# Moving the tile loads of outsb from GpSimd's DMA queue to SyncE's in an attention and FFN kernel on eight cores

## The chip, the cores and the metric

The kernel runs on the 8 cores of one Trainium2 chip. Each core runs the same program on 2 of the 16 batches, and the cores exchange nothing. The metric is the time on the device in microseconds (us), that of the slowest core.

A core has TensorE (PE in the profile), VectorE (DVE), ScalarE (ACT), GpSimd (POOL) and SyncE (SP). Each takes its instructions in order. Transfers between HBM and the core's own memory are issued by SyncE, into the hardware queue q1, or by GpSimd, into the software queue q0; 16 DMA engines serve both. An instruction that waits, a DMA too, holds everything behind it on its engine.

## The reference, cut to what matters

```python
xn = _layernorm(x, axis=-1)                      # x: 16 x 2048 x 1024, float32
# attention-like part, data = xn
sq = jnp.sum(data * data, axis=-1, keepdims=True)
normed = data * jax.lax.rsqrt(jnp.maximum(sq, 1e-12))
sim = jnp.einsum('bnd,bmd->bnm', normed, normed)
counter = jnp.sum(jax.nn.relu(sim), axis=-1, keepdims=True)
counter = jax.nn.softplus(counter @ W1 + b1)     # 2048 x 1024 per batch
a = jnp.concatenate([data, counter], axis=-1) @ W2
# low-rank FFN
P = jnp.einsum('bsd,dr->bsr', xn, U1)            # rank 256
H = jax.nn.gelu(jnp.einsum('bsr,rf->bsf', P, V1) + b1)
f = jnp.einsum('bsr,rd->bsd', jnp.einsum('bsf,fr->bsr', H, U2), V2) + b2
x = x + a + f
```

## The kernel before, in words

The 2048 rows of a batch are cut into 16 tiles `st` of 128 rows (512 KB each) and 4 groups of four tiles. Small helpers return lists of units, each a cost and a function; `mix` interleaves several lists by these costs, and playing the result gives the order of the instructions. `Sched.add` records each instruction with the tiles that it reads and writes, and works out the waits; what is recorded for "SY" is SyncE's queue and what is recorded for "G" is GpSimd's, each in that order.

**Startup (batch 0).** For each group: four tiles of `x` are loaded into `xa`/`xr` on SyncE (L462), one group ahead, and ScalarE takes the sum and the sum of squares (L473, L478), which frees the buffer for the next load. Some 25 small operations (`emit_colmath`, L333 to L376) make mean and scale. Then the same four tiles are loaded again, into `outsb[st % 2]` (`rld`, L741, on GpSimd), VectorE normalizes them (L415 into `ntok`, in group 0 also L445 into `xntok`), TensorE transposes them (L384) and ScalarE copies them out (L396). Blocks of the similarity matrix follow (L494), each reduced on VectorE (L502). The weights come in 18 chunks of 1 MB through two staging buffers `wstage` (L314, on SyncE), and ScalarE (even chunks, L317) or VectorE (odd chunks, L320) casts them. Chunks 0 to 5 are mixed into the startup, 6 to 17 into stage 1 of batch 0.

On SyncE the startup's order is: constants, `xa` tile 0, chunk 0, tiles 1 to 3; tiles 4 to 7; chunk 1; tile 8, chunk 2, tiles 9 to 11; chunk 3; tiles 12 to 15; chunks 4, 5; then chunks 6, 7 and so on. In the order of the list, the loads of outsb (tile n: rld n) stand at these places: rld 0 and 1 after the load of tile 7 and ahead of chunk 1, rld 2 and 3 behind it; rld 4 to 7 between the load of tile 11 and chunk 3; rld 8 and 9 after tile 15, then chunk 4, rld 10 and 11, chunk 5, rld 12 to 15, chunk 6.

**Stages 1 to 5 of each batch.** The rest of the similarity matrix, the FFN (L603, L624, L636), and `fin_units`, which makes an output tile: `gx` loads `x` again into `outsb[st % 2]` (L669, on GpSimd), 19 matmuls for each half add up in a PSUM bank (L677 to L697), VectorE adds the bank onto outsb (L703), and GpSimd stores it (L710). `gx` of tile n waits for the store of tile n-2. On GpSimd the order is store n-1, gx n, and then mostly the load of an `xr` tile (L440). In stages 2 and 3 of batch 0 SyncE loads the tiles of batch 1 into `xa` for their statistics (L462), and in stages 4 and 5 for `nfm` (L409); each waits until its buffer is free. In batch 1 SyncE has no work.

Of the kernel before, what the change touches and what calls it, by code (L numbers as in the profile page):

```python
# [9 lines left out]
AFT = mybir.ActivationFunctionType  # L10
# [6 lines left out]
QLAG = 2  # L17
HBF_N = 4
FIN_ADD_ENG = "V"
CS_ADD_ENG = "V"  # L20
PQ_EVAC_ENG = "V"
CF_POS = 20
# [145 lines left out]
def build_program():  # L168
# [88 lines left out]
    def pool_slot():  # L257
        i = state["pool"] % POOL_N
        state["pool"] += 1
        return pool[i], ("ps", i)  # L260
# [169 lines left out]
        lc, tp = ph1_units2(b, st, slot_buf, slot_key, load_chan, eng, tok)  # L430
        return lc + tp

    def prep_units2(b, st, slot_buf, slot_key, load_chan=None, load_eng="G"):
        p = b % 2
        C = cols
        t = st // 4
        lc = []
        if load_chan is not None:
            def ld():
                A(load_eng, lambda e: e.dma_start(out=slot_buf[:, :],  # L440
                                                  in_=x[b, st * 128:(st + 1) * 128, :]),
                  writes=[slot_key], chan=load_chan, dma=True)
            lc.append((600, ld))
        def cast():
            A("V", lambda e: e.tensor_scalar(out=xntok[st % 4][:, :], in0=slot_buf[:, :],  # L445
                            scalar1=C["invs"][p][:, st:st + 1],
                            scalar2=C["biasB"][p][:, st:st + 1],
                            op0=AluOpType.mult, op1=AluOpType.add),
              reads=[slot_key, ("cmB", p, st)], writes=[("xntok", st % 4)])
        lc.append((600, cast))  # L450
        return lc, [tp_group(xntok[st % 4], ("xntok", st % 4), xnfm[t % 2],
                             ("xnfm", t % 2), st % 4)]
# [34 lines left out]
    def sim_block_unit(b, q, kc, j, nb_, last):  # L487
        def emit():
            bank, bkey = pool_slot()
            vs = vj_slot()  # L490
            state["blkvs", b, q, kc] = vs
            for dc in range(DC):
                A("T", lambda e, dc=dc:
                  e.matmul(bank[:, :],  # L494
                           nfm[:, dc * 2048 + q * 128: dc * 2048 + (q + 1) * 128],
                           nfm[:, dc * 2048 + kc * 512: dc * 2048 + (kc + 1) * 512],
                           start=(dc == 0), stop=(dc == DC - 1)),
                  reads=[("nfm", q // 4), ("nfm", kc)],
                  writes=[bkey], tag=f"sim{b}_{q}_{kc}")
            col = 4 * (q % 4) + j  # L500
            A("V", lambda e:
              e.tensor_scalar(out=vjunk[:, vs * 512:(vs + 1) * 512],  # L502
                              in0=bank[:, :], scalar1=0.0,
                              scalar2=None, op0=AluOpType.max, op1=AluOpType.add,
                              accum_out=cpart[:, col:col + 1]),
              reads=[bkey], writes=[("cp", col), ("vj", vs)])
            if last:
                A("V", lambda e:
                  e.reduce_sum(call[:, q:q + 1], cpart[:, 4 * (q % 4):4 * (q % 4) + nb_],
                               axis=AX.X),  # L510
                  reads=[("cp", 4 * (q % 4) + jj) for jj in range(nb_)],
                  writes=[("call", q)])
        return (4400, emit)
# [150 lines left out]
    def fin_units(b, t):  # L664
        units = []
        for s_ in range(4):
            st = 4 * t + s_
            def gx(st=st):
                A("G", lambda e: e.dma_start(out=outsb[st % 2][:, :],  # L669
                                             in_=x[b, st * 128:(st + 1) * 128, :]),  # L670
                  writes=[("outsb", st % 2)], chan=("QXF", st % 2), dma=True)
            units.append((600, gx))
            for h in range(2):
                def finh(s_=s_, st=st, h=h):
                    bank, bkey = pool_slot()
                    A("T", lambda e:
                      e.matmul(bank[:, :], onesbr[:, :],  # L677
                               b2bf[0:1, h * 512:(h + 1) * 512], start=True, stop=False),
                      reads=[("onesbr",), ("b2bf",)], writes=[bkey], tag=f"Fb2_{b}_{t}_{s_}")
                    for dc in range(DC):  # L680
                        A("T", lambda e, dc=dc:
                          e.matmul(bank[:, :],  # L682
                                   xnfm[t % 2][:, dc * 512 + s_ * 128: dc * 512 + (s_ + 1) * 128],
                                   w2sb[:, dc * 1024 + h * 512: dc * 1024 + h * 512 + 512],
                                   start=False, stop=False),
                          reads=[("xnfm", t % 2), ("w", "w2")],
                          writes=[bkey], tag=f"F{b}_{t}_{s_}")
                    for dc in range(DC):
                        A("T", lambda e, dc=dc:
                          e.matmul(bank[:, :],  # L690
                                   nfm[:, dc * 2048 + t * 512 + s_ * 128: dc * 2048 + t * 512 + (s_ + 1) * 128],
                                   w2sb[:, (8 + dc) * 1024 + h * 512: (8 + dc) * 1024 + h * 512 + 512],
                                   start=False, stop=False),
                          reads=[("nfm", t), ("w", "w2")], writes=[bkey])
                    for rc in range(2):
                        A("T", lambda e, rc=rc:
                          e.matmul(bank[:, :],  # L697
                                   qfm[t % 2][:, rc * 512 + s_ * 128: rc * 512 + (s_ + 1) * 128],
                                   v2sb[:, rc * 1024 + h * 512: rc * 1024 + h * 512 + 512],
                                   start=False, stop=(rc == 1)),  # L700
                          reads=[("qfm", t % 2), ("w", "v2")], writes=[bkey])
                    A(FIN_ADD_ENG, lambda e:
                      e.tensor_tensor(out=outsb[st % 2][:, h * 512:(h + 1) * 512],  # L703
                                      in0=bank[:, :],
                                      in1=outsb[st % 2][:, h * 512:(h + 1) * 512],
                                      op=AluOpType.add),
                      reads=[bkey, ("outsb", st % 2)], writes=[("outsb", st % 2)])
                units.append((9600, finh))
            def store(st=st):
                A("G", lambda e: e.dma_start(out=out[b, st * 128:(st + 1) * 128, :],  # L710
                                             in_=outsb[st % 2][:, :]),
# [16 lines left out]
    for g in range(NT):  # L728
# [8 lines left out]
        for s_ in range(4):  # L737
            st = 4 * g + s_
            rbuf, rkey = outsb[st % 2], ("outsb", st % 2)
            def rld(rbuf=rbuf, rkey=rkey, st=st):  # L740
                A("G", lambda e: e.dma_start(out=rbuf[:, :],  # L741
                                             in_=x[0, st * 128:(st + 1) * 128, :]),
                  writes=[rkey], chan=("QXF", st % 2), dma=True)
            startup.append((600, rld))
            lc, tp = ph1_units2(0, st, rbuf, rkey, load_chan=None, eng=PH1_ENG, evac="S")
            startup.extend(lc)
# [161 lines left out]
```

How the kernel before makes its waits and increments, by code:

```python
    def emit(self, stream, eng, sems):  # L122
        for o in self.streams[stream]:
            if o.drain:
                eng.drain()
            for c, idx in sorted(o.waits.items(), key=lambda kv: str(kv[0])):
                v = self.wait_value(c, idx)
                if v > 0:
                    eng.wait_ge(sems[c], v)
            inst = o.fn(eng)
            if o.marked:
                if inst is None:
                    inst = eng.nop()
                inst.then_inc(sems[o.chan], 16 if o.dma else 1)
# [733 lines left out]
        @block.gpsimd  # L868
        def _(eng):
            sch.emit("G", eng, sems)
            for k in range(3):
                n_store = sch.chan_count.get(("QST", k), 0)
                if n_store:
                    eng.wait_ge(sems[("QST", k)], 16 * n_store)
```

## Time and profile before

| | us |
|---|---|
| median of 2 runs | 1070.17 (1060.68 and 1079.66) |
| the profiled execution | 1062.01 |
| its span on the slowest core (core 4) | 1060.5 |
| the other cores' spans | 1048.9 to 1054.9 |
| mean granted clock of TensorE, core 4 | 0.879 of full speed |

The busy share of an engine is an average over stages with different limits. The chain of waits goes back from the last instruction to what released each step. "Issue" in it is time for which the profile shows no wait. A DMA's time to landing runs from its issue to the semaphore that tells of its end.

### The profile page before, as it was taken

What the parts mean: (1) busy time and instruction counts of PE and PEld (TensorE: products, weight loads), DVE (VectorE), ACT (ScalarE), POOL (GpSimd) and SP (SyncE); (2) the same over time, 40 slices, a digit from 0 to 9 for tenths busy, and PEclk for the clock granted to TensorE, in tenths of its full rate; (3) what the DMA queues carried; (4) which work ended last, traced back from release to release, by engine and by line L of the source; (5) the groups of instructions that cost most, each with busy time, mean ns of one, the idle gap of its engine ahead of it and who ended that gap; (6) DMA issues with size and microseconds to landing.
All of it is one profiled execution on the core that took longest, in us unless ns stands there. A gap on an engine that the chain in (4) does not pass through costs nothing.

```text
span 1060.5 us, 10460 instructions; the slowest of 8 cores (1048.9 to 1060.5 us)
## 1 busy us (share of the span) xinstructions
PE 794.1 (75%) x3592; PEld 344.4 (32%) x3592; DVE 263.8 (25%) x573; ACT 419.9 (40%) x582; POOL 74.0 (7%) x144
## 2 busy tenths in 40 slices
PE   0335566693999399759967985993999399959997
PEld 0212222232444134324433332441344134324442
DVE  1424343331333122321122333322222111111111
ACT  3344522447243724666341001347223623566310
POOL 0000001001000100100000000001000100100001
PEclk9976668896999599959987997996999689969999
DMA  6546434711223223212352221101111112111222
GB/s 188 173 159 214 148 113 143 265 69 40 100 100 119 79 100 120 106 53 80 100 156 83 100 90 49 60 20 41 60 60 61 59 48 72 60 40 40 80 80 100
DMA packets 32486, 101.49 MB, mean 96 GB/s; under 512 B 4401, under 2 KB 9649, under 8 KB 31922
## 3 DMA queue, kind: packets, MB, share of 16 engines
q0 software_dynamic: 16576, 56.65, 15.3%
q1 hardware_dynamic: 15858, 44.17, 13.1%
q8 instruction: 30, 0.49, 0.2%
q14 instruction: 22, 0.18, 0.1%
HBM read 84.01 MB, written 16.78 MB: 95 GB/s over the span
## 4 chain that ended last, share of the span: by engine, by line
PE 66%; ACT 15%; DMA 8%; issue 6%; DVE 4%; SPq 0%; ACTq 0%; DVEq 0%; POOL 0%; POOLq 0%
PE s L494 13%; PE s L682 10%; PE q L636 10%; PE s L690 10%; PE hx L624 5%; PE s L624 5%; PE tb L384 4%; ACT wstage L579 4%; ACT nfm L584 3%; DMA wstage<-W 3%; PE s L697 2%; ACT xnfm L396 2%; PE s L677 2%; ACT nfm L396 2%; DMA outsb<-x 2%
## 5 line engine op out<-in xcount | busy, mean ns | idle before, releaser
L636 PE MATMUL q<-hbf,u2sb 128*128 128x512 bf16 x512 | 156.4, 391 | 29.6 <-ACT hbf L630 29.5
L494 PE MATMUL s<-nfm 128*128 128x512 bf16 x640 | 173.5, 422 | 5.5 <-ACT nfm L396 5.0
L630 ACT ACTIVATE hbf<-s,fb1c 128x512 bf16<-128x512 f32 x128 | 87.8, 686 | 159.9 <-PE s L624 159.7
L630 ACT ACTIVATE hbf<-hx,fb1c 128x512 bf16<-128x512 f32 x128 | 87.8, 686 | 135.2 <-PE hx L624 135.2
L682 PE MATMUL s<-w2sb,xnfm 128*128 128x512 bf16 x512 | 122.3, 382 | 0.0
L703 DVE TENSOR_TENSOR outsb<-s,outsb 128x512 f32<-128x512 f32 x64 | 44.2, 691 | 309.8 <-PE s L697 280.5
L690 PE MATMUL s<-w2sb,nfm 128*128 128x512 bf16 x512 | 121.0, 379 | 0.0
L384 PE MATMUL tb<-identbf,xntok 128*128 128x128 bf16 x384 | 43.7, 284 | 79.4 <-ACT xnfm L396 55.3
L502 DVE TENSOR_SCALAR_CACHE_REDUCE vjunk<-s 128x512 bf16<-128x512 f32 x80 | 55.3, 691 | 190.9 <-PE s L494 190.9
L624 PE MATMUL hx<-pfm,v1sb 128*128 128x512 bf16 x256 | 78.8, 391 | 25.9 <-ACT hbf L630 25.5
L494 PEld LDWEIGHTS s<-nfm 128*128 128x128 bf16 x640 | 65.4, 106 | 94.8 <-issue 39.4
L624 PE MATMUL s<-pfm,v1sb 128*128 128x512 bf16 x256 | 77.2, 383 | 20.4 <-DVE pfm L610 13.5
L636 PEld LDWEIGHTS q<-hbf,u2sb 128*128 128x128 bf16 x512 | 50.7, 100 | 95.3 <-issue 38.8
L384 PE MATMUL tb<-identbf,ntok 128*128 128x128 bf16 x128 | 16.2, 306 | 87.3 <-DVE ntok L415 76.5
L396 ACT COPY nfm<-tb 128x1024 bf16<-128x1024 bf16 x32 | 32.4, 1012 | 119.0 <-PE tb L384 119.0
L690 PEld LDWEIGHTS s<-w2sb,nfm 128*128 128x128 bf16 x512 | 50.1, 98 | 60.4
L682 PEld LDWEIGHTS s<-w2sb,xnfm 128*128 128x128 bf16 x512 | 45.0, 98 | 61.6 <-issue 16.8
L384 PEld LDWEIGHTS tb<-identbf,xntok 128*128 128x128 bf16 x384 | 34.2, 128 | 90.5 <-issue 90.0
L710 POOL DMA_DIRECT2D out<-outsb x32 | 17.3, 541 | 566.3 <-DVE outsb L703 566.3
L396 ACT COPY xnfm<-tb 128x1024 bf16<-128x1024 bf16 x32 | 32.3, 1010 | 55.1 <-PE tb L384 55.1
L579 ACT ACTIVATE wstage<-s,b1c,w1c 128x512 f32<-128x512 f32 x64 | 49.7, 777 | 5.3
L624 PEld LDWEIGHTS hx<-pfm,v1sb 128*128 128x128 bf16 x256 | 24.1, 99 | 60.3 <-issue 34.7
(86 smaller groups left out, 584.5 us busy)
## 6 DMA issues: line engine op xcount, KB each, us to landing
outsb<-x POOLq DMA_DIRECT2D x48, 512.0 KB, 4.9
xa<-x SPq DMA_DIRECT2D x40, 512.0 KB, 3.9
out<-outsb POOLq DMA_DIRECT2D x32, 512.0 KB, 3.0
xr<-x POOLq DMA_DIRECT2D x28, 512.0 KB, 5.8
wstage<-W SPq DMA_DIRECT2D x8, 1024.0 KB, 6.8
wstage<-U SPq DMA_DIRECT2D x5, 1024.0 KB, 7.8
wstage<-V SPq DMA_DIRECT2D x5, 1024.0 KB, 7.7
xr<-x SPq DMA_DIRECT2D x8, 512.0 KB, 5.5
```

The costliest lines, as they stand in the source:

```text
L384: e.transpose(tb[:, dc * 128:(dc + 1) * 128], src[:, dc * 128:(dc + 1) * 128], identbf[:, :]),
L396: e.copy(dst.rearrange("p (c f) -> p c f", c=8)[:, :, st * 128:(st + 1) * 128], tb[:, :].rearrange("p (c f) -> p c f", c=8)),
L494: e.matmul(bank[:, :], nfm[:, dc * 2048 + q * 128: dc * 2048 + (q + 1) * 128], nfm[:, dc * 2048 + kc * 512: dc * 2048 + (kc + 1) * 512], s ...
L502: e.tensor_scalar(out=vjunk[:, vs * 512:(vs + 1) * 512], in0=bank[:, :], scalar1=0.0, scalar2=None, op0=AluOpType.max, op1=AluOpType.add, ...
L579: e.activation(out=e512[dc % 2][:, :], in_=bank[:, :], func=AFT.Exp, scale=w1c[:, dc:dc + 1], bias=b1c[:, dc:dc + 1]),
L584: e.activation(out=nfm[:, dc * 2048 + t * 512: dc * 2048 + (t + 1) * 512], in_=e512[dc % 2][:, :], func=AFT.Ln, bias=1.0, scale=1.0),
L624: e.matmul(bank[:, :], v1sb[:, c * 4096 + fc * 128:c * 4096 + (fc + 1) * 128], pfm[t % 2][:, c * 512:(c + 1) * 512], start=(c == 0), stop= ...
L630: e.activation(out=hbf[fc % HBF_N][:, :], in_=bank[:, :], func=AFT.Gelu_apprx_tanh, scale=1.0, bias=fb1c[:, fc:fc + 1]),
L636: e.matmul([q0, q1][rc][:, :], u2sb[:, fc * 256 + rc * 128: fc * 256 + (rc + 1) * 128], hbf[fc % HBF_N][:, :], start=(fc == 0), stop=(fc = ...
L682: e.matmul(bank[:, :], xnfm[t % 2][:, dc * 512 + s_ * 128: dc * 512 + (s_ + 1) * 128], w2sb[:, dc * 1024 + h * 512: dc * 1024 + h * 512 + ...
L690: e.matmul(bank[:, :], nfm[:, dc * 2048 + t * 512 + s_ * 128: dc * 2048 + t * 512 + (s_ + 1) * 128], w2sb[:, (8 + dc) * 1024 + h * 512: (8 ...
L703: e.tensor_tensor(out=outsb[st % 2][:, h * 512:(h + 1) * 512], in0=bank[:, :], in1=outsb[st % 2][:, h * 512:(h + 1) * 512], op=AluOpType.add),
```

## The change

The loads of outsb, `rld` (16) and `gx` (32), are recorded for SyncE instead of GpSimd, at the same place of the order. `rld` gets a semaphore of its own (QXO). The rest of the diff changes nothing in the program that is built: `RELU_SPLIT` and `FIN_SPLIT` are 0, so the added branches aren't taken and `finh` calls its two halves in turn, with the same cost in `mix`; the new default of `load_eng` is not used, since each caller that loads passes "G".

```diff
+RELU_SPLIT = 0
+FIN_SPLIT = 0
-    def prep_units2(b, st, slot_buf, slot_key, load_chan=None, load_eng="G"):
+    def prep_units2(b, st, slot_buf, slot_key, load_chan=None, load_eng="SY"):
...
             def gx(st=st):
-                A("G", lambda e: e.dma_start(out=outsb[st % 2][:, :],
+                A("SY", lambda e: e.dma_start(out=outsb[st % 2][:, :],
                                              in_=x[b, st * 128:(st + 1) * 128, :]),
                   writes=[("outsb", st % 2)], chan=("QXF", st % 2), dma=True)
...
-                units.append((9600, finh))
+                if FIN_SPLIT:
+                    units.append((4800, finA))
+                    units.append((4800, finB))
+                else:
+                    def finh(finA=finA, finB=finB):
+                        finA(); finB()
+                    units.append((9600, finh))
...
             def rld(rbuf=rbuf, rkey=rkey, st=st):
-                A("G", lambda e: e.dma_start(out=rbuf[:, :],
-                                             in_=x[0, st * 128:(st + 1) * 128, :]),
-                  writes=[rkey], chan=("QXF", st % 2), dma=True)
+                A("SY", lambda e: e.dma_start(out=rbuf[:, :],
+                                              in_=x[0, st * 128:(st + 1) * 128, :]),
+                  writes=[rkey], chan=("QXO", st % 2), dma=True)
```

## Rows read from the trace of the kernel before

**Rows 1.** The page: busy times and its chain by engine.
```profile
PE 794.1 (75%) x3592; PEld 344.4 (32%) x3592; DVE 263.8 (25%) x573; ACT 419.9 (40%) x582; POOL 74.0 (7%) x144
PE 66%; ACT 15%; DMA 8%; issue 6%; DVE 4%; SPq 0%; ACTq 0%; DVEq 0%; POOL 0%; POOLq 0%
```

**Rows 2.** Waits of the whole span: us in total, times, longest.
```profile
DVE outsb L703 <- DMA outsb<-x: 29.3, 5, 7.3
ACT u2sb L317 <- DVE u2sb L320: 26.2, 1, 26.2
DVE ntok L415 <- DMA outsb<-x: 16.5, 7, 5.7
```

**Rows 3.** Busy time by stretch: length, then each engine's, clock, DMA, GB/s.
```profile
215.00:1016.00 801.00, 659.60 (x2998) 285.43 (x2997) 187.07 (x370) 334.38 (x462) 55.77 (x107) 0.89 0.21 73
1016.00:1054.00 38.00, 37.00 (x164) 14.98 (x161) 6.92 (x10) 1.52 (x3) 4.23 (x8) 1.00 0.31 111
```

**Rows 4.** The chain in order of time: start, length, what.
```profile
4.14 12.81 DMA wstage<-U
106.55 5.75 DMA outsb<-x
136.72 3.47 DMA outsb<-x
630.29 6.55 DMA xr<-x
```

**Rows 5.** DMA of 0 to 30 us: GB/s by 0.75 us, issues with time to landing.
```profile
GB/s 0 0 29 92 36 78 372 321 264 314 254 338 288 296 345 279 274 261 306 318 333 258 236 208 147 82 33 0 0 0 0 180 382 137 109 224 218 224 289 208
outsb<-x POOLq DMA_DIRECT2D x2, 512.0 KB, 6.5
wstage<-V SPq DMA_DIRECT2D x1, 1024.0 KB, 8.8
```

**Rows 6.** VectorE in order of time: start, length, operation, [idle before, releaser].
```profile
33.55 0.81 DVE L415 TENSOR_SCALAR ntok<-outsb,c_scaleA,c_biasA 128x1024 bf16<-128x1024 f32 x1
37.90 1.23 DVE L320 CAST v1sb<-wstage 128x2048 bf16<-128x2048 f32 x1 [2.81 <-DMA wstage<-V]
77.43 1.53 DVE L415 TENSOR_SCALAR ntok<-outsb,c_scaleA,c_biasA 128x1024 bf16<-128x1024 f32 x2
105.18 1.53 DVE L415 TENSOR_SCALAR ntok<-outsb,c_scaleA,c_biasA 128x1024 bf16<-128x1024 f32 x2
112.46 0.81 DVE L415 TENSOR_SCALAR ntok<-outsb,c_scaleA,c_biasA 128x1024 bf16<-128x1024 f32 x1 [5.74 <-DMA outsb<-x]
```

**Rows 7.** SyncE's queue in order of time: start, until the last issue, load.
```profile
28.98 0.43 SPq L314 DMA_DIRECT2D wstage<-V  x1
72.86 0.43 SPq L314 DMA_DIRECT2D wstage<-V  x1
97.42 50.62 SPq L314 DMA_DIRECT2D wstage<-U  x4
```

**Rows 8.** DMA issues of 70 to 73 us.
```profile
wstage<-V SPq DMA_DIRECT2D x1, 1024.0 KB, 6.6
```

**Rows 9.** SyncE's queue, 270 to 345 us: the loads for batch 1's statistics.
```profile
275.21 63.23 SPq L462 DMA_DIRECT2D xa<-x  x7
```

**Rows 10.** GpSimd in order of time: stores and loads of outsb.
```profile
302.66 0.54 POOL L710 DMA_DIRECT2D out<-outsb  x1 [18.91 <-DVE outsb L703]
303.19 0.53 POOL L669 DMA_DIRECT2D outsb<-x  x1
629.76 0.54 POOL L710 DMA_DIRECT2D out<-outsb  x1 [15.02 <-DVE outsb L703]
```

**Rows 11.** The page's list of DMA issues: median us to landing.
```profile
outsb<-x POOLq DMA_DIRECT2D x48, 512.0 KB, 4.9
xa<-x SPq DMA_DIRECT2D x40, 512.0 KB, 3.9
out<-outsb POOLq DMA_DIRECT2D x32, 512.0 KB, 3.0
```

More of the change, by code:

```diff
@@ L500, in emit @@
             col = 4 * (q % 4) + j
[L501 to L506, printed above, removed]
+            state["relu_rr"] = state.get("relu_rr", 0) + 1
+            if RELU_SPLIT and state["relu_rr"] % 2 == 0:
+                A("S", lambda e:
+                  e.activation(out=vjunk[:, vs * 512:(vs + 1) * 512], in_=bank[:, :],
+                               func=AFT.Relu, accum_out=cpart[:, col:col + 1]),
+                  reads=[bkey], writes=[("cp", col), ("vj", vs)])
+            else:
+                A("V", lambda e:
+                  e.tensor_scalar(out=vjunk[:, vs * 512:(vs + 1) * 512],
+                                  in0=bank[:, :], scalar1=0.0,
+                                  scalar2=None, op0=AluOpType.max, op1=AluOpType.add,
+                                  accum_out=cpart[:, col:col + 1]),
+                  reads=[bkey], writes=[("cp", col), ("vj", vs)])
             if last:
@@ L673, in fin_units, with finA @@
             for h in range(2):
-                def finh(s_=s_, st=st, h=h):
+                share = {}
+                def finA(s_=s_, st=st, h=h, share=share):
                     bank, bkey = pool_slot()
+                    share["b"] = (bank, bkey)
                     A("T", lambda e:
@@ L687, in finh, with finB @@
                           writes=[bkey], tag=f"F{b}_{t}_{s_}")
+                def finB(s_=s_, st=st, h=h, share=share):
+                    bank, bkey = share["b"]
                     for dc in range(DC):
@@ L707, in finh @@
                       reads=[bkey, ("outsb", st % 2)], writes=[("outsb", st % 2)])
-                units.append((9600, finh))
+                if FIN_SPLIT:
+                    units.append((4800, finA))
+                    units.append((4800, finB))
+                else:
+                    def finh(finA=finA, finB=finB):
+                        finA(); finB()
+                    units.append((9600, finh))
             def store(st=st):
```

## The prediction, made before the change ran

> **What bounds the kernel now.** I read the page first: TensorE is busy for 75% of the span and makes 66% of the chain; DMA is 8% of it [rows 1]. The list of waits says where outsb's loads are waited for: VectorE loses 16.5 us to them in the startup (L415) and 29.3 us at its adds (L703) [rows 2]. Then the busy time by stretch: from 215 us on TensorE is busy 82% of the time, and in the last stage, 1016 to 1054 us, for 37.0 of 38 us [rows 3], although most of the 29.3 us lie there. So the adds' wait costs TensorE nothing there. The chain in order of time shows what the DMAs do cost: at the start chunk 0, 12.81 us; a load of outsb once in each startup group; and at the change of batch a load of xr, 6.55 us [rows 4].
>
> **The start.** Two loads of outsb go out from GpSimd at about 1.6 us and land in 6.5 us while chunk 0 (issued 4.14, 12.81 us to landing, ScalarE waits for it) shares the DMA engines with them; the rate from 4.5 us on is about 300 GB/s [rows 4, 5]. With the change they stand behind the load of tile 7, so 2 x 0.52 MB leave the first 17 us: 1.05 / 0.30 = 3.5 us earlier for chunk 0, and for ScalarE's work behind it. The upper bound is 4.0 (at 262 GB/s, near the lowest of the 17 slices from 4.5 us); the lower bound is 0, if chunk 0 with its rows of 1 KB is bound by itself. I take 3.5, since the rate is level for the whole time, as if bytes counted.
>
> **Group 0.** What gained 3.5 is given back. SyncE's order puts rld 0 and 1 ahead of chunk 1, whose cast (L320) VectorE must do before it normalizes tile 1. Chunk 1 was issued at 28.98, took 8.8 us and was waited for (2.81 us, cast at 37.90) [rows 5 to 7]. Now 1.05 MB stand ahead of it: +4.0 us at 0.26 MB/us (the slices before 30 us show 0.22 to 0.29), less about 0.8 because rld 2, once beside it, is now behind it, less 3.5: chunk 1 lands 0.3 us earlier. rld 0 itself: cast 0 stood at 33.55 [rows 6] and could start at 30.1, but rld 0 lands about 31; this is hidden in the wait for chunk 1. Group 0 ends **0.3 us earlier** (3.2 later if the start brings nothing).
>
> **Group 1.** rld 4 and 5 were prefetched; now they are issued behind tile 11 where chunk 3 was (72.86). The bytes are those of chunk 3, which took 6.6 us [rows 7, 8], so they land at about 77.5 and 79.5, less the 0.3. Cast 4 stood at 77.43, cast 5 right behind it [rows 6]: casts 4 and 5 slip by 0.1 and 1.3 us against before. The transposes go at 2.4 us a tile, so cast 5 isn't late for its own. rld 6 is issued at the end of cast 4 without the 0.5 us that GpSimd takes for it. I put group 1 at **-0.1** (bounds -0.5 and +1.5).
>
> **Group 2.** rld 8 and 9 are issued at about 96.4, ahead of chunks 4 and 5, which left at 97 [rows 7]; cast 8 wants its tile at 105.18 [rows 6]: hidden, with 3 us to spare. The gain is rld 10: issued 106.55, 5.75 us to landing, since chunk 5 was in flight; cast 10 waited 5.74 us for it [rows 4, 6]. Now chunk 5 stands behind rld 11. Only chunk 4 is ahead; it lands at about 108 instead of sharing with chunk 5, and rld 10 2 us behind it, at 110 instead of 112.3: **-2.0** (bounds 0 and -2.5; the floor is a load alone, 3.47 us [rows 4]).
>
> **Group 3.** rld 12 and 13 are early. rld 14 takes 3.47 us [rows 4] as before, issued some 0.5 us sooner after its cast: **-0.2**. Chunks 6 and 7 are now held behind rld 14 and 15, which wait for casts 12 and 13: chunk 6 leaves at 134 instead of 112 and takes up to 8 us. Its cast on ScalarE stood at about 146, and behind it ScalarE waits 26.2 us for VectorE anyway [rows 2]. Nothing.
>
> Sum of the startup: -0.3 - 0.1 - 2.0 - 0.2 = **-2.6 us**.
>
> At this point the Trainium skill (DMA: Bandwidth & Descriptors, "Latency and other measured facts") gives a first byte after about 0.6 us from the hardware path and about 1 us from the software path. By it the four gated loads of the startup would bring 4 x 0.4 = 1.6 us, and the startup would come to -4.2. The page's medians, 4.9 us for outsb and 3.9 for xa [rows 11], have the same sign but mix loads alone with loads in company; the sum above has nothing of this but the 0.5 us of GpSimd's issue.
>
> **Stages 1 to 5.** gx n went out on GpSimd right behind store n-1 (302.66 and 303.19 [rows 10]), although the buffer was free since store n-2 had landed. Now it goes some 16 us sooner, and the waits at L703 mostly vanish. That is worth nothing to TensorE in the last stage, as shown, and between 215 and 1016 us only one of the five waits lies, 7.3 us at most [rows 2]; the chain has no load of outsb after the one at 136.72. Gain 0 (bound: 1 us, the idle rest of the last stage [rows 3]).
> What queues behind gx on SyncE: the loads of xa in stages 2 to 5 of batch 0. In 63.23 us 7 of them went out, about 10 us apart [rows 9]. gx 3 must wait for store 1, 302.66 + 3.0 to land = 305.7 [rows 10, 11]; the load behind it, tile 6, went at about 275 + 4 x 10.5 = 317. 11 us to spare; the other gx have 7 us or more. Nothing. In stage 1, gx 0 and 1 join chunk 17 and two xa loads at 206 us; they stand behind the chunk, and what they delay is wanted 15 us later or more.
> The xr loads stay on GpSimd behind the stores, which didn't move. They lose one companion each. gx 12 leaves the row of 8 xa loads at 544 to 562 us and goes behind it: -0.2.
>
> **The change of batch.** The last store of batch 0 goes at 629.76, and behind it two xr loads for which VectorE, and with it TensorE, waits (6.55 us in the chain) [rows 4, 10]. Batch 1's gx 1, once at 760, waits for that very store: it goes at 633 now, into the same DMAs. 0.52 MB at 0.3 MB/us is 1.75 us, of which most finds the xr loads nearly through: **+0.5** (bounds 0 and 1.75).
>
> **Sum:** -2.6 - 0.2 + 0.5 = -2.3 us; 1062.01 - 2.3 = **1059.7 us**. The profiled execution is near the faster of the two runs shown, 1060.68; the median of 1070.17 stands halfway to one of 1079.66.
>
> **The rivals.**
> *All cancels (0.20).* The loads are hidden either way; 1062. For it: startup groups 0, 1 and 3 move by tenths. Against it: cast 10's 5.74 us.
> *The weights become late (0.19).* The other side. Chunk 0 is bound by its own rows, the 3.5 us don't come, and chunk 1 is late by the full 3.2 us in front of cast 1; with group 1's bound of 1.5 and groups 2 and 3 giving back 2.0, the change of batch 1.0: 1062 + 3.7 = 1065.7. It decides where chunk 1 lands later than 37.8. Against it: the level 300 GB/s.
> The Trainium skill (same page, "Queues, rings and completion order", on arbitration) says that a DMA engine takes turns between queue rows and works through one row in order. By it the moved loads lose their own turn and stand behind all that SyncE has sent, which is this rival's way.
> *The startup's waits for outsb go (0.05).* If loads on q1 land at once, the 16.5 us [rows 2] and the 3.5 go: 1042. Against it: two buffers, so every second load still waits for a cast.
> *The adds' waits were TensorE's after all (0.02).* -29.3 [rows 2]: 1033. Against it: 37.0 of 38 us busy.
> *SyncE's queue stalls (0.04).* A gx waits for its store while the loads for ScalarE's statistics stand behind it; 14 gx at 2 us each: 1090. It decides where the margin of 11 us above is gone.
>
> **How the numbers follow.** The forecast has 0.50. It, the cancelling and the late weights lie between 1057 and 1066 and make 0.89, all within 2% (about what a measurement of this kernel can tell from no change). What widens the range is not the mechanism but which execution is taken: the two runs shown are 19 us apart. So from 1053 to 1077: below, all lower bounds (0.5 at the start, 0.4, 0.5, 0.5 and 1.0, some 3 us) off 1059.7 and 3 more for an execution that is 0.3% faster, as the cores' spans differ; above, the slower of the runs shown less 2.3. Faster by over 2% has 0.03, from the rivals with 20 us and more; slower 0.04; the same 0.93.
>
> **What would show it.** ScalarE's first cast at 13 to 14.5 us instead of 17; chunk 1's cast still near 37.6; cast 10 at about 109.5 to 110; TensorE's last block of group 3 some 2.6 us earlier; no DMA wait at L703 and TensorE's busy time unchanged; xr's wait at the change of batch not shorter. The forecast is wrong if chunk 0 lands no earlier, if ScalarE waits for an xa load in stages 2 and 3, or if TensorE idles less after 215 us.

## The result: 0.75% slower, and most of it lies behind the last add

| | before | after |
|---|---|---|
| median, us | 1065.18 (12 runs) | 1071.42 (13 runs) |
| ratio of the times | | 1.0075 (95% interval 1.0052 to 1.0098) |
| the profiled execution | 1062.01 | 1069.68 |
| its span on the slowest core | 1060.5 | 1067.9 |
| mean span of the 8 cores | 1056.2 (29 runs) | 1062.6 (12 runs) |

The ratio and the mean spans leave out the runs in which the cores of one die showed a lower clock, while the medians have all runs. The 29 runs are those of the kernel before made beside e1 and e2, below, since the runs beside the changed kernel have only the slowest core's time on record for the kernel before. The change costs about 8 us on the slowest core and 6.4 us on the mean core. It was forecast to win 2.3 us. The measured 1071.42 us lies inside the stated 1053 to 1077 us all the same, but only because the range was made wide for the spread between runs: the direction was wrong.

The page of the changed kernel shows what the prediction said of the engines: TensorE's busy time and the chain are nearly as before (TensorE has 66% of the chain in both, ScalarE 15% and now 13%, DMA 8% and now 10%), VectorE's adds have no DMA among what ends their idle time, and GpSimd is left with 96 of its 144 instructions ([rows 1, 11] are the lines of before). Columns of the third line: busy, mean ns; idle before it, and what ended most of that.

```profile
PE 789.1 (74%) x3526; PEld 344.8 (32%) x3592; DVE 263.6 (25%) x573; ACT 419.9 (39%) x582; POOL 48.0 (4%) x96
PE 66%; ACT 13%; DMA 10%; issue 6%; DVE 4%; SPq 0%; ACTq 0%; DVEq 0%; POOL 0%; POOLq 0%
L716 DVE TENSOR_TENSOR outsb<-s,outsb 128x512 f32<-128x512 f32 x64 | 44.2, 691 | 310.1 <-PE s L710 310.1
outsb<-x SPq DMA_DIRECT2D x48, 512.0 KB, 4.5
```

The 29.3 us of waits at the adds [rows 2] are gone, and the time is longer all the same. Nothing of the above shows where it went, since the engines' busy times and the chain by line stop at real work. What the engine queues did at the very end stands in the list of the instructions of the program's last line (`with nc.Block()`): operation, count, ns, start in us. First the kernel before, then the changed one; the last DRAIN is GpSimd's in both.

```profile
L855 DVEq DRAIN  x1: 703/703/703, 1053.3 to 1053.3; - x1
L855 POOLq DRAIN  x1: 2756/2756/2756, 1057.5 to 1057.5; - x1
```
```profile
L874 DVEq DRAIN  x1: 703/703/703, 1055.9 to 1055.9; - x1
L874 POOLq DRAIN  x1: 7574/7574/7574, 1060.1 to 1060.1; - x1
```

GpSimd's DRAIN starts when the last store has landed. It took 2.756 us and now takes 7.574 us, on each of the 8 cores to the ns. From the end of the last add to the end of the span it was 6.53 us before and is 11.33 us after. So 4.8 of the 6.4 us are one instruction that no line of the diff names. The other 1.6 us lie ahead of it. VectorE's timeline of the changed kernel's startup answers to [rows 6] (start, length, operation, idle before and releaser):

```profile
34.86 0.81 DVE L417 TENSOR_SCALAR ntok<-outsb,c_scaleA,c_biasA 128x1024 bf16<-128x1024 f32 x1 [3.31 <-DMA outsb<-x]
39.34 1.23 DVE L322 CAST v1sb<-wstage 128x2048 bf16<-128x2048 f32 x1 [2.94 <-DMA wstage<-V]
108.12 1.53 DVE L417 TENSOR_SCALAR ntok<-outsb,c_scaleA,c_biasA 128x1024 bf16<-128x1024 f32 x2
114.34 0.81 DVE L417 TENSOR_SCALAR ntok<-outsb,c_scaleA,c_biasA 128x1024 bf16<-128x1024 f32 x1 [4.68 <-DMA outsb<-x]
```

and its chain in order of time to [rows 4] (start, length):

```profile
4.15 10.84 DMA wstage<-U
27.97 11.28 DMA wstage<-V
109.02 5.15 DMA outsb<-x
138.42 4.84 DMA outsb<-x
636.68 6.12 DMA xr<-x
```

Chunk 0 lands 2.0 us sooner here, chunk 1 takes 11.28 us instead of 8.8 and its cast starts 1.4 us later, and the load of tile 10 takes 5.15 us instead of 5.75. A single profile can't carry a difference of 1 us: the mean cores of two executions of the same instructions (the kernel before and f3, below) were 2 us apart at the end of the startup and 4 us at the last add. So the startup is read from all profiles with the start and stage 1 of before (before, e2, e8, f2 to f5: 7 kernels, 56 cores) and with the changed ones (after, e1, e4, e6, e12: 5 kernels, 40 cores), as means over the cores. Here ± is one standard error, the cores taken as independent:

| VectorE's instruction | before | change |
|---|---|---|
| statistics of group 0 (needs chunk 0's cast out of the way) | 27.77 us | -2.38 ± 0.22 |
| cast of chunk 1 | 37.23 | +1.13 ± 0.27 |
| normalizing tile 10 | 110.36 | +1.2 ± 0.5 |
| last sums of the startup | 156.1 | +1.6 ± 0.6 |
| first evacuation of stage 1's FFN, behind ScalarE's long wait | 169.5 | +0.7 ± 0.6 |
| last add | 1048.2 | +0.8 ± 1.0 |

### The profile page after: what moved, and what is told of

Its sections match the earlier page's. It is cut to its first block, busy times and chain, and to the rows that moved or that the text cites. A ratio compares the mean times of both kernels' runs of the same rounds, so it can differ in the third digit from the quotient of the medians.

```text
span 1067.9 us, 10393 instructions; the slowest of 8 cores (1052.5 to 1067.9 us)
## 1 busy us (share of the span) xinstructions
PE 789.1 (74%) x3526; PEld 344.8 (32%) x3592; DVE 263.6 (25%) x573; ACT 419.9 (39%) x582; POOL 48.0 (4%) x96
## 4 chain that ended last, share of the span: by engine, by line
PE 66%; ACT 13%; DMA 10%; issue 6%; DVE 4%; SPq 0%; ACTq 0%; DVEq 0%; POOL 0%; POOLq 0%
PE s L496 12%; PE s L693 11%; PE s L703 10%; PE q L645 10%; PE s L633 5%; PE hx L633 5%; PE tb L386 4%; ACT wstage L588 4%; DMA wstage<-W 3%; PE s L710 3%; ACT nfm L593 3%; ACT xnfm L398 2%; DMA outsb<-x 2%; PE s L688 2%; DMA wstage<-V 2%
## 5 line engine op out<-in xcount | busy, mean ns | idle before, releaser
L645 PE MATMUL q<-hbf,u2sb 128*128 128x512 bf16 x498 | 152.9, 391 | 30.2 <-ACT hbf L639 29.5
L496 PE MATMUL s<-nfm 128*128 128x512 bf16 x622 | 168.2, 417 | 8.7 <-ACT nfm L398 6.1
```

The costliest lines, as they stand in the source:

```text
L496: e.matmul(bank[:, :], nfm[:, dc * 2048 + q * 128: dc * 2048 + (q + 1) * 128], nfm[:, dc * 2048 + kc * 512: dc * 2048 + (kc + 1) * 512], s ...
L645: e.matmul([q0, q1][rc][:, :], u2sb[:, fc * 256 + rc * 128: fc * 256 + (rc + 1) * 128], hbf[fc % HBF_N][:, :], start=(fc == 0), stop=(fc = ...
```

## The experiments

In what follows a "software DMA" is one that GpSimd issues, and "body" is the mean core's span over the runs that the ratio uses, less the time from the end of the last add to the end of the span in that kernel's profile (one value per kernel, the slowest core's; the cores agree within 0.05 us in most kernels and within 0.8 us in all). "Against before" takes the runs of the kernel before made beside the same experiment. The standard errors of the mean spans are 0.2 to 0.8 us, and 1.5 us in f5; f3 and f4 are single runs. The variants are made from one source with five switches:

```diff
+RLD_ENG = "SY"   # rld, the loads of outsb in the startup
+GX_ENG = "SY"    # gx, the loads of outsb in fin_units
+XR_ENG = "G"     # loads of xr
+ST_ENG = "G"     # stores of out
+CR_ENG = "G"     # copies crow4 -> cscr
```

| kernel | DMAs on GpSimd | last DRAIN, us | last add to end | ratio to before | body against before |
|---|---|---|---|---|---|
| before | 140 | 2.756 | 6.53 | 1 | 0 |
| after | 92 | 7.574 | 11.33 | 1.0075 | +1.6 |
| e1 startup only | 124 | 10.187 | 13.96 | 1.0090 | +0.2 |
| e2 output only | 108 | 8.881 | 12.64 | 1.0059 | +0.9 |
| e3 no software DMA | 0 | 0.041 | 3.05 | 1.0042 | +7.4 |
| e4 stores too | 60 | 4.961 | 7.98 | 1.0032 | +0.2 |
| e5 prefetch kept | 92 | 7.574 | 11.35 | 0.9929 | -12.4 |
| e6 40 pads | 132 | 7.574 | 11.33 | 1.0076 | +1.8 |
| e7 hardware only | 4 | 0.383 | 3.38 | 0.9892 | -6.4 |
| e8 before, 128 | 128 | 10.514 | 14.28 | 1.0084 | -0.5 |
| e9 prefetch order only | 92 | 7.574 | 11.34 | 0.9998 | -4.9 |
| e10 chunk order only | 140 | 10.272 | 14.05 | 1.0021 | -5.0 |
| e11 hardware but stage 1 | 12 | 1.036 | 4.05 | 0.9852 | -13.6 |
| e12 drain midway | 92 | 0.376 | 4.14 | 1.0010 | +2.6 |
| f2 before, drain midway | 140 | 0.702 | 4.49 | 0.9979 | +0.3 |
| f3 before again | 140 | 10.269 | 14.05 | one run, 1074.12 us | +1.3 |
| f4 one semaphore | 140 | 2.021 | 5.80 | one run, 1064.81 us | -2.1 |
| f5 own semaphore | 140 | 9.861 | 13.63 | 1.0060 | 0.0 |

### The two halves of the change, each alone

e1: `GX_ENG = "G"`.

> Only the 16 startup loads of outsb (rld) go to SyncE; the 32 loads of the output tiles (gx) stay on GpSimd. Theory A (two places: the startup is 2 us later because the weight chunks and the prefetched tiles now stand in one queue, and GpSimd's drain behind the last store lasts 7.57 us instead of 2.76): startup +2.0 us as in the full change; the drain answers to the software DMAs of the program, 128 here against 144 before and 96 after, so it is neither value if a count sets it (4.4 us on a straight line between the two), and ratio 1.002 to 1.004. Theory B (the steady stages lose through the queue's order, the drain is a by-product of the early gx loads): startup +2.0 and drain 2.76 us, ratio 1.002.

Measured: 1.0090 (1.0056 to 1.0124), DRAIN 10.187 us. Both theories named a shorter one (4.4 and 2.76 us) and a smaller ratio.

e2: `RLD_ENG = "G"`.

> Only the 32 loads of the output tiles (gx) go to SyncE; the startup is as before. Theory A: startup 0.0 us, adds no longer wait for outsb, the last drain between 2.76 and 7.57 us or 7.57 itself (5.97 on a straight line in the number of software DMAs, 112 here), everything between 215 us and the last add unchanged within 0.5 us: ratio 1.003 to 1.005. Theory B: 2 us or more are lost between 215 us and the last add as well.

Measured: 1.0059 (1.0031 to 1.0086). Here too the DRAIN of 8.881 us is longer than either theory had it. Each half alone costs about as much as both together. The table says why: with 124 and 108 DMAs left on GpSimd the DRAIN takes 10.187 and 8.881 us, while the bodies are within 1 us of before. The first hypothesis, that the startup's order or SyncE's queue carries the loss, fell here.

### No DMA on GpSimd, and the stores moved too

e3: all five switches on "SY".

> Every DMA of the program goes to SyncE, the stores, the xr loads and the small cscr copies too; GpSimd issues none. If the drain grows as the number of software DMAs falls (a straight line through 144: 2.76 and 96: 7.57), it would be 17 us here and the ratio 1.02. If it is spent on software transfers that it has yet to clear, there is nothing to clear: under 0.5 us, and the end of the program comes 7 us sooner than after the change: ratio about 1.002 minus what the one queue costs. What the one queue may cost: loads of xa wait behind stores in stages 2 to 5 of batch 0.

Measured: 1.0042 (1.0017 to 1.0067). The DRAIN is 41 ns. But the body is 7.4 us longer, and about 9 us of loss come between 168 and 205 us, in stage 1 of batch 0, where ScalarE waits 27.3 us for a chunk of U (e7 and e11, below, show why).

e4: `ST_ENG = "SY"`.

> The full change and the 32 stores on SyncE as well; GpSimd keeps 28 xr loads and 32 small copies. On the straight line the drain is 10.8 us, by the theory of transfers not yet cleared it is what 28 large and 32 small ones leave, no more than in the full change (7.57) if it never cleared any, less than 7.57 otherwise. The wait for the last store is then SyncE's landing as seen by GpSimd; ratio 1.00 to 1.01.

Measured: 1.0032 (1.0006 to 1.0059): 60 DMAs on GpSimd, 4.961 us.

With n DMAs issued on GpSimd and n at most 128, the DRAIN follows one line through 0, 4, 12, 60, 92, 108, 124 and 128: 0.06 + 0.0817 n us, within 0.01 us from 60 on and 0.02 below that. The kernel before, with 140, is far off it (11.5 by the line, 2.756 measured).

### The 128th DMA

e6: the changed kernel with 40 loads of 4 bytes on GpSimd at the start, all on one semaphore; nothing uses what they load.

```diff
+    for i in range(N_PAD):                      # N_PAD = 40
+        A("G", lambda e, i=i: e.dma_start(out=padsb[0:1, i:i + 1], in_=b2[0:1, i:i + 1]),
+          writes=[("pad", i)], chan="QPAD", dma=True)
```

> The full change plus 40 DMAs of 4 bytes on GpSimd at the very start, into a scratch row that nothing reads; GpSimd is idle there. This adds work and no saving. Software DMAs: 132 instead of 92. So far the drain lasted 4.96, 7.57, 8.88, 10.19 us with 60, 92, 108, 124 of them, 0.0817 us each whatever their size, and 2.76 us with 140, where GpSimd stops for 2.59 us behind its 128th. If the count is all, 107 are cleared at the 128th and 25 are left: drain 2.1 us, and the kernel with 40 more transfers ends 5.5 us sooner than the changed one, ratio 1.002. If the drain answers to bytes, to time or to the gx loads, it lasts 7.57 us or more (10.8 us by the slope): ratio 1.0075 to 1.011.

Measured: 1.0076 (1.0053 to 1.0098), DRAIN 7.574 us as without the pads. 132 DMAs, and the time of 92. The 2.1 us of the count were missed; the number is the rival's, but what follows gives it another reason.

e8: the kernel before with the last 12 loads `gx` of batch 1 on SyncE, so that 128 are left.

> The kernel before, but for the last 12 of the 32 gx loads (batch 1, tiles 4 to 15), which go to SyncE: 128 software DMAs instead of 140. If the count rules, GpSimd never comes to its 129th, nothing is cleared, and the drain is 0.06 + 128 x 0.0817 = 10.5 us, 7.8 us more than before: ratio 1.007. If the clearing comes with the 128th itself, 21 are left and the drain lasts 1.8 us: ratio 0.999. The work up to the last add does not move.

Measured: 1.0084 (1.0058 to 1.0110), the body 0.5 us shorter, DRAIN:

```profile
L881 POOLq DRAIN  x1: 10514/10514/10514, 1054.2 to 1054.2; - x1
```

Twelve fewer software DMAs make the end 7.8 us longer. It is as if up to 128 every software DMA stays on the books, and with the 129th a part is cleared. "Books" and "cleared" are names for what fits; the profile shows only the DRAIN and the stop. GpSimd's timeline of the kernel before shows when: a stop of 2.59 us ahead of its 129th DMA, for which the profile has no releaser.

```profile
986.62 0.53 POOL L669 DMA_DIRECT2D outsb<-x  x1 [2.59 <-issue]
```

At that stop 140 - 33 = 107 DMAs must have been cleared, for the DRAIN of 2.756 is the line's at n = 33. In e6 it was 40, which are the pads. What decides the number was open. That it isn't the count alone came out in e10 below, meant for something else: the same 140 software DMAs in the same order, and a DRAIN of 10.272 us.

f3: the instructions of the kernel before, each the same on its engine, made from the source of the variants.

> The kernel before once more, instruction for instruction the same on each engine, built from the source in which all the variants are made. Theory A, the number of software DMAs that is cleared between the 128th and the 129th is a property of the program: stop of 2.59 us, last DRAIN 2.76 us again on every core. Rival B, it goes by the moment at which the 129th is issued or by chance: another stop and another last DRAIN, such as the 0.44 and 10.27 us of e10_chunk_order_only, which has the same software DMAs in the same order.

Measured: a stop of 0.44 us, and then

```profile
989.05 0.53 POOL L683 DMA_DIRECT2D outsb<-x  x1 [0.44 <-issue]
...
L879 POOLq DRAIN  x1: 10269/10269/10269, 1062.1 to 1062.1; - x1
```

Theory A as stated, "a property of the program", looked refuted, and chance looked likely. It is neither: this source has one thing of the diff that the kernel before has not. The 16 startup loads `rld` have semaphores of their own (QXO), where the kernel before let them share QXF with `gx`. By the line, 15 were cleared, and the 15th software DMA is the last one on the even QXO. The 40th in e6 is the last on the pads' semaphore, and the 107th in the kernel before is the last cscr copy on the even QTN. In all three it is the first DMA behind which, among the first 128, no other uses its semaphore (none does later in the program either, so the two forms of the rule can't be told apart here). Two kernels tested that rule where it says something definite:

```diff
# f4
-                  chan=("QTN", t % 2), dma=True)
+                  chan=("QTN", 0), dma=True)
# f5
-                  chan=("QTN", t % 2), dma=True)
+                  chan=("QTF", 0) if b == 0 and t == 0 else ("QTN", t % 2),
+                  dma=True)
```

> The kernel before, with the cscr copies of all tiles on one semaphore instead of two in turn. Three programs with over 128 software DMAs so far: the last DRAIN says that 107, 15 and 40 of the first 128 were cleared at the 129th. Theory A, cleared is everything up to the first software DMA that is the last one on its semaphore among those 128: in the kernel before that is the 107th (the last cscr copy on the even semaphore), in f3_before_again and e10 the 15th (the last outsb load of the startup on a semaphore of its own), in e6 the 40th (the last pad). Here the first such is the 116th, an xr load: stop 0.09 + 116 x 0.0234 = 2.8 us, 24 left, last DRAIN 0.061 + 24 x 0.0817 = 2.02 us. Rival B, the number has nothing to do with the semaphores of the cscr copies: last DRAIN 2.76 us as before.

> The kernel before, with the four cscr copies of t=0 in batch 0 (the 17th to 20th software DMA) on a semaphore that nothing else uses. No instruction, size or order is changed. Theory A (cleared is everything up to the first software DMA that is the last one on its semaphore): 20 cleared, 120 left, stop 0.09 + 20 x 0.0234 = 0.56 us, last DRAIN 0.061 + 120 x 0.0817 = 9.87 us instead of 2.76, ratio to the kernel before 1.005 to 1.008. Rival B: last DRAIN 2.76 us, ratio 1.000 within 0.002.

Measured, f4 and then f5, the 129th DMA and the last DRAIN:

```profile
990.37 0.53 POOL L669 DMA_DIRECT2D outsb<-x  x1 [2.79 <-issue]
...
L855 POOLq DRAIN  x1: 2021/2021/2021, 1061.0 to 1061.0; - x1
```
```profile
984.44 0.53 POOL L670 DMA_DIRECT2D outsb<-x  x1 [0.56 <-issue]
...
L856 POOLq DRAIN  x1: 9861/9861/9861, 1057.3 to 1057.3; - x1
```

Both as the rule said, to 0.01 us, stop and DRAIN. In f5 nothing but a semaphore's name is changed, and the mean core is 7.1 us slower (1057.6 and 1064.6 us; the ratio of this noisier pair is 1.0060, 0.9996 to 1.0124). So the mean core's difference has a standard error of 1.7 us, but the DRAIN's 7.1 us are the same on all cores. Five different numbers fit the rule now (15, 20, 40, 107, 116), two of them forecast; why it is so no run shows.

### The DRAIN moved to where it costs nothing

e12: the changed kernel; f2: the kernel before. Both get one line more.

```diff
             if b + 1 >= NB and sg == 5:
+                A("G", lambda e: e.drain())
                 play(fin_units(b, 3))
```

> The changed kernel with one instruction more: GpSimd drains its queue once in batch 1, before the store of tile 12 (at about 1016 us), while TensorE has some 38 us of work left. Theory A, the last DRAIN costs about 0.08 us for each software DMA issued since the queue was last cleared: the drain in the middle takes about 7.3 us (88 DMAs) beside other work, the last one 0.061 + 4 x 0.0817 = 0.39 us instead of 7.57, the end of the program comes 7.2 us earlier, and the ratio to the kernel before is 1.000 to 1.002 instead of 1.0075. Rival B, the length goes by all software DMAs of the program and not by those since the last clearing: last DRAIN 7.57 again, ratio 1.007. Rival C, the store of tile 12 or its successors come late behind the drain and the adds of tiles 14 and 15 wait for a free outsb: last DRAIN 0.39, but the part before the last add longer by 1 to 4 us.

> The kernel before with one instruction more: GpSimd drains its queue once in batch 1, before its load of tile 12 into outsb, as e12_drain_midway has it in the changed kernel. Theory A (the DRAIN costs 0.06 us and 0.08 us for each software DMA still on the books, and those of the first 128 that were cleared at the 129th are off them): the drain in the middle takes 2 to 2.5 us, the last one 0.061 + 8 x 0.0817 = 0.71 us instead of 2.76, and the ratio to the kernel before is 0.997 to 0.999. So against e12_drain_midway (1.001) the change without its drain is within 0.4 per cent of nothing. Rival B, the first drain delays tile 12's load and the add of tile 12 waits for it: ratio 1.000 to 1.003.

The two DRAINs of e12:

```profile
L867 POOLq DRAIN  x1: 7811/7811/7811, 1022.7 to 1022.7; - x1
...
L875 POOLq DRAIN  x1: 376/376/376, 1063.8 to 1063.8; - x1
```

The 7.8 us lie beside TensorE's work in the last stage, the last DRAIN is the line's for 4 DMAs, and the ratio goes from 1.0075 to 1.0010 (0.9993 to 1.0027). f2: the last one 0.702 us (8 DMAs, by the line 0.71), the one in the middle 4.0 us where 2 to 2.5 were expected (the store of tile 11 is issued as it starts and lands 2.9 us into it; no load is on the way; what makes it 4.0 is open), ratio 0.9979 (0.9957 to 1.0001). So the end makes 4.8 us of the loss, shown by moving it and not only read: with the end levelled the change is 1.0010 / 0.9979 = 1.003, and the mean core's bodies are 2.3 ± 0.5 us apart. Against the changed kernel e12's body is 1.0 ± 0.6 us longer, which is not clear of the noise; the last ten adds wait for TensorE alone on all 8 cores, so rival C has nothing in the trace.

### What the startup could have given

e5: the changed kernel with rld 0 and 1 issued right behind the first four tile loads, and rld 4g+4 and 4g+5 right behind group g's casts.

```diff
+    startup.append(rld_unit(0))
+    startup.append(rld_unit(1))
     pend_cs = []
...
+        if g < NT - 1:
+            startup.append(rld_unit(4 * g + 4))
+            startup.append(rld_unit(4 * g + 5))
```

> The full change, but with the startup's loads of outsb at other places in SyncE's order: tiles 0 and 1 right behind the first four loads of xa and xr, and tiles 4g+4 and 4g+5 right behind the casts of group g instead of behind the next group's statistics loads. Nothing else moves; 92 software DMAs, so the last drain is again 7.57 us. If the startup of the changed kernel suffers from the order in the one queue, chunk 0 lands 2.3 us sooner than before (14.5 us) and chunk 1 no later than before, and the work up to the last add is 2 to 4 us shorter than in the changed kernel: ratio to before 1.002 to 1.005. If the order does not matter, the ratio is the changed kernel's, 1.0075.

Measured: 0.9929 (0.9908 to 0.9950), the body 12.4 us shorter. The expectation's "nothing else moves" was not so. The moved units carry their cost into `mix`, and weight chunk 2 came out ahead of the load of tile 8. ScalarE's timeline has the effect: the cast of chunk 2 in the kernel before, and in e5.

```profile
64.28 1.90 ACT L317 CAST v1sb<-wstage 128x2048 bf16<-128x2048 f32 x1 [8.25 <-DMA wstage<-V]
```
```profile
54.56 1.88 ACT L324 CAST v1sb<-wstage 128x2048 bf16<-128x2048 f32 x1
```

e9 and e10 take the two apart. e9 gives the moved units the cost 0 and leaves empty units of the old cost in the old places; e10 is the kernel before with the empty units in the new places, so that only chunk 2 moves.

> As e5_prefetch_kept (changed kernel, with the outsb loads of tiles 0 and 1 issued right behind the first four tile loads and the loads of tiles 4g+4 and 4g+5 right behind group g's casts), but the weight chunks keep the places that they have in the kernel before: chunk 2 is issued behind tile 8's load again. In e5 the weight chunk 2 had also moved ahead of tile 8's load (issued at 44.2 instead of 56.0 us), which its expectation did not say. Theory A, the gain of e5 is mostly chunk 2's place (ScalarE's cast of chunk 2 waits for it at about 56 to 64 us when it is issued late): that wait of 6 to 8 us is back, the part before the last add is 2 to 4 us shorter than in the changed kernel, and the ratio to the kernel before is 1.002 to 1.006. Rival B, the gain of e5 is the earlier outsb loads: ratio 0.993 as e5, with the wait at 56 to 64 us back but swallowed later. GpSimd's last DRAIN 7.57 us by both (92 software DMAs).

> The kernel before, all outsb loads on GpSimd, with one thing moved: weight chunk 2 is issued ahead of the load of tile 8 on SyncE instead of behind it. Theory A (chunk 2's place is most of e5's gain): ScalarE's wait for chunk 2 near 56 to 64 us goes, the part before the last add is 5 to 8 us shorter, ratio 0.993 to 0.996. Rival B (e5's gain comes from the earlier outsb loads): ratio 1.000 within 0.002, the time that the earlier chunk wins being lost to a later outsb load. GpSimd's last DRAIN 2.76 us by both, since the 140 software DMAs are as before.

Measured: e9 0.9998 (0.9978 to 1.0019), body -4.9; chunk 2's wait is back, 6.39 us of it. e10 1.0021 (1.0007 to 1.0036), body -5.0. Both theories were too simple. Chunk 2's place is worth 5.0 us in the kernel before and 7.5 us on top of e9. The earlier loads are worth 6.5 us against the changed kernel (+1.6 to -4.9), more than the 2 to 4 that A gave them; e9's ratio missed A's 1.002 to 1.006 for that. And e10's ratio missed 0.993 to 0.996 though its body did what A said, since the DRAIN took back 7.5 us. It took the body and the end apart to see either.

### All on SyncE but what gates the weights

e7: e5 with `XR_ENG`, `ST_ENG` and `CR_ENG` on "SY", and the four xr loads of stage 1 of batch 0 on GpSimd.

> As the run before the last (tile loads early in SyncE's order), and stores, cscr copies and all xr loads on SyncE too, but for the four xr loads of stage 1 of batch 0, which stay on GpSimd: with no software DMA at all these four stood behind the weight chunks and 8 us were lost between 168 and 205 us. 4 software DMAs: drain 0.4 us, 7.2 us less than after the change and 2.4 less than before. If both causes are right, the work up to the last add is 2 to 3 us shorter than before and the end 3 us: ratio 0.993 to 0.996. If the stores in the queue hold the xa loads back, 1.00.

Measured: 0.9892 (0.9874 to 0.9910), better than the 0.993 to 0.996 expected. But the expectation put e3's loss in stage 1 down to the four xr loads, and with them back on GpSimd nearly all of it is there: in e3 8.9 us go between 168 and 179 us, in e7 8.5. In the profile the mean core was 13.7 us ahead of before at 168 us and 5.3 us ahead at 179. SyncE's queue (start, until the last issue) shows the reason, and ScalarE's timeline its effect:

```profile
148.99 5.71 SPq L573 DMA_DIRECT2D cscr<-crow  x4
154.75 8.96 SPq L321 DMA_DIRECT2D wstage<-U  x3
```
```profile
161.37 1.90 ACT L324 CAST u2sb<-wstage 128x2048 bf16<-128x2048 f32 x1 [26.61 <-DMA wstage<-U]
169.74 1.90 ACT L324 CAST u2sb<-wstage 128x2048 bf16<-128x2048 f32 x1 [6.48 <-DMA wstage<-U]
```

The cscr copies wait for VectorE, and three weight chunks that could have gone at 126 us stand behind them until 154.75. e11 puts the eight copies of t=0 and t=1 of batch 0 back on GpSimd.

```diff
+            early = b == 0 and t <= 1
-                A(CR_ENG, lambda e, qi=qi:
+                A("G" if early else CR_ENG, lambda e, qi=qi:
...
-                  chan=("QTN", t % 2), dma=True)
+                  chan=("QTG" if early else "QTN", t % 2), dma=True)
```

> As e7_hardware_only (e5's order, tile stores, xr loads and cscr copies on SyncE, but the four xr loads of stage 1 of batch 0 on GpSimd), with the eight cscr copies of tiles t=0 and t=1 of batch 0 on GpSimd too: 12 software DMAs. In e7 the kernel lost about 9 us between 168 and 192 us against e5. Theory A, that loss is SyncE's queue standing at the cscr copies of t=0, which wait for VectorE while weight chunks stand behind them: the loss goes, GpSimd's last DRAIN is 0.061 + 12 x 0.0817 = 1.04 us, and the ratio to the kernel before is 0.980 to 0.985. Rival B, the loss has another cause (the tile stores or loads on SyncE): ratio 0.989 to 0.991, with the loss at 168 to 192 us kept.

Measured: 1047.16 us, 0.9852 (0.9833 to 0.9870), the fastest of all. SyncE's queue and the end:

```profile
126.39 12.85 SPq L321 DMA_DIRECT2D wstage<-U  x3
...
L889 POOLq DRAIN  x1: 1036/1036/1036, 1043.8 to 1043.8; - x1
```

The chunks go at 126 us again, the loss between 168 and 192 us is gone (11.0 us ahead at 168 us, 11.1 at 179), and the DRAIN is the forecast 1.04 us. The ratio is just above the 0.980 to 0.985 of theory A. Not all of the gain belongs to the queues: of the 13.6 us in the body some 5 to 7.5 us are chunk 2's place (e10, e5 against e9), which needs no load moved.

## Why the prediction was wrong, step by step

- **The end of the program. The step that failed is one that the sum did not have.** It went from the start to the change of batch and took what lies behind the last add as unchanged, without a word on it. The prediction looked at GpSimd's DMAs only for what each issue costs (0.5 us). Their number came back at the end: -48 DMAs should have made the DRAIN shorter, but 140 was above 128 and 92 below, so the clearing at the 129th fell away too. +4.8 us, shown by e8, f5, e12 and f2.
- **The start** (-3.5, bounds 0 and -4.0). The mechanism was right, the term too large: -2.4 us (VectorE's statistics; chunk 0's own landing moved from 17.1 to 14.7 on the mean core). The loads' bytes left the stretch and chunk 0 won less than they would take at 0.30 MB/us; why, no run shows.
- **Group 0** (-0.3). Wrong in sign: chunk 1's cast came 1.1 us later, since 1.1 us less was won ahead of it, and rld 0 and 1 in front of it cost 3.5 us where the sum had 3.2. Of the 3.5, chunk 1 took 2.5 us longer to land, and 1.0 us is SyncE's time for the two issues, a term that the sum did not have. It landed at 38.3 us on the mean core, and the prediction had named 37.8 as the point from which the rival *the weights become late* decides. That rival held for the startup in mechanism and in small size: a loss of 1.6 us at its end and not 3.7. The rule of the Trainium skill that it rested on (DMA: Bandwidth & Descriptors, "Queues, rings and completion order") agrees with chunk 1's 11.28 us to landing in the profile of after, 8.8 before [rows 5]; on the mean core of the pooled profiles it is 10.5 and 8.0. That bears on the order within one row; no run here tests the turns between rows.
- **Group 1** (-0.1, up to +1.5). Within its bounds: VectorE's sums ended 1.0 us late in group 0 and 1.5 us late in group 1, so it added 0.5. Casts 4 and 5 (so the prediction names the normalizing of tiles 4 and 5) came 1.9 and 2.3 us late.
- **Group 2** (-2.0, bounds 0 and -2.5). Not there. On the mean core of the pooled profiles the load of tile 10 took 5.2 us to landing where it had taken 5.0, and tile 10 was normalized 1.2 us late, after 1.5 us at the end of group 1. Chunk 4 landed at 108.1 us, as the sum had it, but the load landed 3.3 us behind it and not 2. The sum let the load lose its company. Before, chunk 4 had landed (104.4 us) and chunk 5 had 2.4 us to go when tile 10's load was issued; now rld 8 and 9 hold chunk 4 back by 3.7 us, and chunk 4 has 1.9 us to go. One chunk took the other's place; that this is the whole reason is read from the traces and not tested. The landing at 112.3 us was also the slowest core's. The mean core's was 110.2, so the 110 of the sum was hardly a gain there.
- **Group 3** (-0.2). Nothing measurable.
- **Chunks 6 and 7** (0). Right: held back, and swallowed by ScalarE's long wait, 24.5 us instead of 26.2 [rows 2]. That wait also takes up much of what the startup lost: from +1.6 at 156 us to +0.7 at 169.
- **Stages 1 to 5** (0) and **SyncE's queue**. Right. The waits at the adds vanished and TensorE gained nothing: busy for 37.49 of the last 38 us, 37.0 before [rows 3]. No load stalled behind a `gx`: between 260 and 600 us VectorE waits 9.9 us for tiles of xa, 11.4 before, and ScalarE not at all.

```profile
1018.00:1056.00 38.00, 37.49 (x163) 15.26 (x164) 6.76 (x11) 2.06 (x3) 2.13 (x4) 1.00 0.26 97
```

- **The change of batch** (+0.5). The load of xr took 6.12 us, 6.55 before [rows 4]; the pooled profiles show +0.5 from batch 0's last add to batch 1's first, with a standard error of about 1 us, so they can't tell +0.5 from 0.

The sum was -2.3. Measured on the mean core are +1.6 ahead of the end and +4.8 behind the last add. The other rivals, with 20 us and more, did not come. Two things stay open. The slowest core lost about 1.5 us more than the mean one, which no run explains. And the +1.6 is +0.8 ± 1.0 by the pooled profiles and +2.3 ± 0.5 between e12 and f2; the traces place it in the startup, but not to a single wait.

## What to carry to other kernels

A DMA moved from one queue to another has a price at the end of the program too: look at the engine queues' last instructions, and not only at the last real work. Here each software DMA cost 0.08 us in GpSimd's last DRAIN, and one `drain()` of GpSimd while TensorE was the bound took that out of the time. When many loads share one in-order queue, put ahead of the weights only those loads that wait for nothing: e7 and e11 differ in that alone, for eight small copies, and e11's body is 7.2 us shorter. And price a wait from all cores and by what else is in flight when the load goes out, not from the slowest core alone.

## What the runs showed of the hardware that was not expected

- GpSimd's DRAIN at the end took 0.06 + 0.0817 us for each DMA issued from it and not cleared, from 0 to 128 DMAs. The size didn't count: e11 has eight cscr copies of 512 bytes more than e7, and its DRAIN is 0.653 us longer, 0.0816 for each; the changed kernel has 32 stores of 512 KB more than e4, and its DRAIN is 2.613 us longer, 0.0817 for each. All transfers but the last store had long landed.
- At the 129th DMA GpSimd stopped and cleared a part of the first 128: 15 in 0.44 us, 20 in 0.56, 107 in 2.59 and 116 in 2.79 to 2.80 (the numbers follow from the DRAIN's line), or 0.09 + 0.0234 us each. Clearing one there takes less than a third of what it costs in the DRAIN.
- How many were cleared followed the semaphores: everything up to the first DMA behind which its semaphore was used no more among the 128. Two numbers of five were forecast by that.
- SyncE's DMAs left nothing of the kind: with all 212 DMAs on SyncE (e3) its own last DRAIN took 0.09 to 0.13 us, with 120 of them (after) 0.09 to 0.12, and GpSimd's in e3 0.041.
